# Macaron block with expert-choice feed-forward on one Trainium2 core: the first expert's weight halves made on ScalarE and GpSimd during the threshold search

## What is computed

```python
x = x + 0.5 * ffn(layernorm(x))
x = x + attention(layernorm(x))
x = x + 0.5 * ffn(layernorm(x))

# ffn (8 experts, 1024 hidden), "expert choice":
xn     = rmsnorm(x) * norm_weight
probs  = softmax(xn @ router_w.T + router_b)
gates, idx = top_k(probs.T, cap)          # cap = 2048 rows for each expert
hmid   = gelu(xn[idx] @ fc1_w[e].T + fc1_b[e])
ye     = hmid @ fc2_w[e].T + fc2_b[e]
out    = scatter_add(ye * gates) / scatter_add(gates)
```

## Time and profile before

| | us |
|---|---|
| median of 3 runs | 2071.78 (2070.72 to 2072.58) |
| the profiled execution | 2071.05 |
| its span, from first to last instruction | 2069.2 |
| PE busy | 1951.3 (94%) |
| DVE busy | 1449.0 (70%) |
| ACT busy | 1398.8 (68%) |
| POOL busy | 1259.4 (61%) |

### The profile page before, as it was taken

The page is one execution under the profiler, slowest core; times in us unless marked ns, Lnnn a source line. Parts: engine busy times, 40 slices in busy tenths (PEclk is TensorE's granted clock), DMA queues, the critical chain, the costliest instruction groups (busy, mean ns, idle before and its releaser), DMA issues. The chain is left out here.

```text
span 2069.2 us, 42505 instructions
## 1 busy us (share of the span) xinstructions
PE 1951.3 (94%) x15382; PEld 1352.3 (65%) x15382; DVE 1449.0 (70%) x4271; ACT 1398.8 (68%) x2680; POOL 1259.4 (61%) x1437
## 2 busy tenths in 40 slices
PE   8858999999999999799999999669999999999997
PEld 6534666666666666577777777435666666666665
DVE  7778777777777765488899998677555555656542
ACT  8635676766767676578888787455576676666663
POOL 8224887777777776644444442027877676767674
PEclk9979999999999999999999999989999999999999
DMA  9943565646565545655555554234655555646453
GB/s 289 346 123 92 114 101 91 106 89 131 85 108 92 100 76 69 116 134 154 159 159 163 135 150 116 85 77 105 107 115 89 107 108 87 131 85 106 71 77 36
DMA packets 361744, 242.33 MB, mean 117 GB/s; under 512 B 228928, under 2 KB 348992, under 8 KB 361280
## 3 DMA queue, kind: packets, MB, share of 16 engines
q1 hardware_dynamic: 304192, 172.34, 31.7%
q0 software_dynamic: 57344, 67.29, 22.4%
HBM read 121.03 MB, written 84.93 MB: 100 GB/s over the span
## 5 line engine op out<-in xcount | busy, mean ns | idle before, releaser
L1273 DVE SCALAR_TENSOR_TENSOR hid_l<-hf,hid_h 128x512 f16<-128x512 f32 x512 | 352.3, 699 | 341.4 <-ACT hid_h L719 340.0
L1494 PE MATMUL ps<-w_h,hid_h 128*128 128x256 f16 x2048 | 559.2, 273 | 0.0
L1495 PE MATMUL ps<-w_l,hid_h 128*128 128x256 f16 x2048 | 559.1, 273 | 0.0
L1496 PE MATMUL ps<-w_h,hid_l 128*128 128x256 f16 x2048 | 558.9, 273 | 0.0
L1494 PE MATMUL ps<-xt,w_h 128*128 128x512 f16 x1024 | 389.8, 381 | 19.4 <-ACT hf L820 14.3
L820 ACT ACTIVATE hf<-ps,b 128x512 f32<-128x512 f32 x512 | 345.1, 674 | 78.5 <-PE ps L1496 72.1
L1496 PE MATMUL ps<-xt,w_l 128*128 128x512 f16 x1024 | 389.9, 381 | 0.0
L1495 PE MATMUL ps<-xt,w_h 128*128 128x512 f16 x1024 | 389.7, 381 | 0.0
L719 ACT ACTIVATE ys<-yb,weight 128x256 f32<-128x256 f32 x256 | 128.0, 506 | 342.6 <-DVE yb L1291 336.2
L719 ACT ACTIVATE hid_h<-hf 128x512 f16<-128x512 f32 x512 | 322.5, 630 | 16.2
L606 POOL DMA_INDIRECT weight<-gate_d,gate_at x256 | 257.7, 1007 | 84.1 <-issue 76.5
(11 more groups left out here) (289 smaller groups left out, 3818.1 us busy)
## 6 DMA issues: line engine op xcount, KB each, us to landing
w_st<-fc_t SPq DMA_DIRECT2D x32, 1024.0 KB
xin<-x SPq DMA_DIRECT2D x32, 512.0 KB, 6.1
xa<-x_d SPq DMA_DIRECT2D x32, 512.0 KB, 4.6
out<-x SPq DMA_DIRECT2D x32, 512.0 KB, 5.2
z_d<-z SPq DMA_DIRECT2D x32, 512.0 KB, 6.1
xt<-xs SPq DMA_TRANSPOSE x256
weight<-gate_d,gate_at POOLq DMA_INDIRECT x256, 2.4
b_st<-fc_b SPq DMA_DIRECT2D x16, 128.0 KB
```

The costliest lines, as they stand in the source:

```text
L1273: dve.scalar_tensor_tensor(hid_l[:, n % 2, f, :], hf[:, f % HF, :], HS, hid_h[:, n % 2, f, :], ALU.mult, ALU.subtract).then_inc(s_hl, 1)
L1494: pe.matmul(dst, lh, rh, start=first, stop=False)
L1495: pe.matmul(dst, lh, rl, start=False, stop=False)
L1496: return pe.matmul(dst, ll, rh, start=False, stop=last)
```

## The change

The high halves of expert E0 are made by ACT inside the search: in rounds 8 and 9 the two parts of `fc1`, in rounds 10 to 13 the four parts of `fc2`, each behind that round's count. The low halves of E0 are made by POOL, as the first thing of its part of the layer, with two instructions for each part: a product by the scale into the loaded weights in place (linked, so POOL waits for its end), and a difference with the high half. The six copies leave ACT's program after the search, and the six low halves of E0 leave DVE's. The other experts are as before.

```diff
+    CONVERT = 8
@@ gpsimd
+            def first_lows(layer):
+                E = NE * layer
+                for k in range(KD):
+                    pool.wait_ge(s_w1h, KD * E + k + 1)
+                    steps.link(pool.tensor_scalar(w1_st[:, k, :], w1_st[:, k, :], nws[:, k:k + 1], None, ALU.mult))
+                    pool.tensor_tensor(w1_l[:, E % 2, k, :], w1_st[:, k, :], w1_h[:, E % 2, k, :], ALU.subtract).then_inc(s_w1, 1)
+                for h in range(4):
+                    pool.wait_ge(s_w2h, 4 * E + h + 1)
+                    part = slice(h * KF // 4, (h + 1) * KF // 4)
+                    steps.link(pool.tensor_scalar(flat(w2_st[:, part, :]), flat(w2_st[:, part, :]), WS, None, ALU.mult))
+                    pool.tensor_tensor(flat(w2_l[:, E % 2, part, :]), flat(w2_st[:, part, :]), flat(w2_h[:, E % 2, part, :]),
+                                       ALU.subtract).then_inc(s_w2, 1)
...
+            first_lows(0)
             ffn_rows(0, xf, x1_d)
...
+            first_lows(1)
             ffn_rows(1, z_d, outf)
@@ scalar, route
                     if i == 2:
                         copy(flat(p_r[:, :, :]), flat(ps[0][:, :, :])).then_inc(s_prr, 1)
+                    if CONVERT <= i < CONVERT + KD:
+                        w1_hi(NE * layer, i - CONVERT)
+                    if CONVERT + KD <= i < CONVERT + KD + 4:
+                        w2_hi(NE * layer, i - CONVERT - KD)
@@ scalar, ffn
                 act.activation(warm[:, :], nws[:, 0:1], ACT.Gelu)
-                for k in range(KD):
-                    w1_hi(E0, k)
-                for h in range(4):
-                    w2_hi(E0, h)
@@ vector, ffn
                 count_slots(0, E0, 0)
-                w1_lo(E0, 0)
                 tiles(0, E0, 1, NC)
                 count_slots(0, E0, 1)
                 rows_stats(N0, 0, 2)
-                if layer == 0:
-                    w1_lo(E0, 1)
                 rows_shift(N0, 0, 2)
                 rows_stats(N0, 2, TG)
                 rows_lo(N0, 0, 2)
-                if layer == 1:
-                    w1_lo(E0, 1)
...
                 choice_2(layer)
-                for h in range(4):
-                    w2_lo(E0, h)
                 rows_stats(N0 + 1)
```

More of the change, by code:

```diff
@@ L756, in _, with w1_hi, w2_hi @@
                     exponents(0, (g - 16) // 10)
+            def w1_hi(E, k):
+                if k == 0:
+                    act.wait_ge(s_w1d, 16 * (E + 1))
+                    wait(act, s_h, KF * NC * (E - 1))
+                copy(w1_h[:, E % 2, k, :], w1_st[:, k, :], scale=nws[:, k:k + 1]).then_inc(s_w1h, 1)
+            def w2_hi(E, h):
+                if h == 0:
+                    act.wait_ge(s_w2d, 16 * (E + 1))
+                    wait(act, s_y, TG * NC * (E - 1))
+                part = slice(h * KF // 4, (h + 1) * KF // 4)
+                copy(w2_h[:, E % 2, part, :], w2_st[:, part, :], scale=WS).then_inc(s_w2h, 1)
             def route(layer):
@@ L823, in gelu @@
                     copy(hid_h[:, n % 2, f, :], hf[:, f % HF, :], scale=HS).then_inc(s_hh, 1)
[L825 to L836, removed]
                 def y_out(n, t):
```

## The result

The changed kernel takes 2088.22 us, median of 4 runs (2086.22 to 2088.40), against 2072.18 (2070.72 to 2072.95, 4 runs) for the kernel before on the same chip: a ratio of 1.0075 with a 95% interval from 1.0059 to 1.0091. It is 16 us slower. The forecast was 2092, with a range from 2077 to 2103 and 0.88 on slower, so time and sign came as forecast. Part of that is luck: POOL worked half as long again as I had put down and held less of the loop than I had assumed, and the two errors nearly cancelled. The profiled execution has a span of 2086.4 us, 17.2 above before.

A forecast was written before the change was run, and what follows sets the result against it. The search's DVE and PE loop bounds its second half, PE nearly all the rest. On the profiled 2071.05 us, +22.0 stalls +3.0 clock -4.3 gain = 2091.75; with the median 0.73 above that execution, about 2092, range 2077 to 2103.

The forecast's parts named there:

- What bounds the kernel: In the search's second half one loop through DVE and PE sets the time, 2.67 us a round; elsewhere PE is nearly full.
- ACT's part: Six copies, 4.7 us a layer, fit ACT's idle 1.43 us in each search round; cost on the loop 0.
- POOL's length: POOL's products and differences beside the search take 13.5 us a layer, and their length alone delays nothing.
- rival (d): POOL is still in the low halves when the rows are listed after the search, so gathers are late; chance 0.01.
- What POOL does to DVE: In the search loop, POOL instructions reading SBUF hold some DVE forms until their end: 11.0 us a layer, 22.0 for both.
- the walk: Laying POOL's work on search rounds: round 8 +1.0, round 9 +4.4, rounds 10 to 13 +1.4 each; 11.0 us a layer.
- rival (c): POOL's product in the search costs as much as two-input arithmetic: 15.7 us a layer, 2102 in all; chance 0.11.
- The clock: PE idles in stretched search rounds and its clock drops: 0.3 us for each of five rounds, 3.0 in all.
- The gain: DVE loses the low halves behind the search: 1.1 and 2.5 us in layer 0, 0.7 in layer 1, 4.3 together.
- Next late are the second group's transposes: In layer 0, without `w2_lo` before the second group's statistics, 2.5 us is gained, as the transposes move with it.
- (a): POOL's instructions don't hold the search loop, so only the gain is left: 2067.5, faster by 0.2%; chance 0.10.
- (b): Only `short` and `cand` are held in the search, the masks pass: 6.8 us a layer, 2081 to 2084; chance 0.16 with mixtures.

The follow-up runs named there:

- e1_high_only: Changed kernel's high halves by ACT inside the search, but low halves left on DVE as in the kernel before, nothing new for POOL: 2071.95 us, ratio 1.0001.
- e5_price: Kernel before plus a test behind its end, timing POOL's product and difference alone and beside short DVE instructions: run once, 2140.41 us.
- e7_roots_sooner: e6_lows_in_wait with POOL's roots of the second group moved ahead of the third group's last two gathers: 2069.64 us, ratio 0.9995.
- after_again: The changed kernel run again, unaltered, for a second profile: 2089.97 us, ratio 1.0083.
- e6_lows_in_wait: Against the kernel before: high halves by ACT in the search, low halves by DVE in its waits for PE there, nothing for POOL: 2070.72 us, ratio 0.9997.
- e8: Changed kernel with ACT making the products too, POOL only the six differences, fc1's high halves moved to rounds 3 and 5: 2090.09 us, ratio 1.0083.
- e3_differences: e1_high_only plus POOL's six differences in each layer, written to an idle tile that nothing reads: 2086.80 us, ratio 1.0074.

## Why the prediction was right, and which of its steps were not

**What bounds the kernel, and ACT's part: right.** The loop of the search was the place: the searches take 19.7 us more (9.25 + 10.42), the whole span 17.2. ACT's copies cost 0 (e1_high_only).

**POOL's length: wrong for the product.** Difference 2.13 and 1.17 forecast, 2.12 and 1.15 to 1.21 measured. Product 1.05 and 0.62 forecast, 2.93 and 1.49 measured, above even the upper bounds of 2.34 and 1.17. The mis-sized term is the product's price. I had taken the slope of a cast, "since it has one input as they have". e5_price shows what the number of inputs does not tell: the multiplication costs 2.8 us where the copy costs 1.04. POOL works 20.9 us a layer instead of 13.5. It ends at 130.58, still 2.5 us before `thr_m`, so rival (d) stayed away, with less room than forecast.

**What POOL does to DVE: right in kind, wrong in one half.** The differences hold `short`, `cand` and the masks' form for their whole length, as the two rows of the trace before had it. The products hold these forms only in parts. Round by round against the forecast: round 8 3.54 (3.7 forecast), round 9 5.13 (7), round 10 4.60 and round 12 4.62 (4), round 11 3.46 (4), round 13 2.97 (4). Round 9 was over-priced: its first difference started after the masks and not in front of them, since the product before it was 1.9 us longer, and it fell on `short`. At the true length of the products and with the whole of each held, the walk would have exceeded rival (c)'s 15.7 us a layer (an argument from the walk, not a run). What was measured is 9.25 and 10.42. The mis-sized product (+7.4 us of POOL work) and the hold assumed whole took each other out.

**The clock: right in kind, and of the forecast's size or a little above.** Rounds 10 to 12 of layer 0 ran at 0.57, 0.50 and 0.69, where before had 0.63 and 0.82 in rounds 11 and 12 (the first in the earlier trace rows). In three rounds the slow clock can be read without a held mask beside it: PE's sums took 1.82 us in round 10 of layer 0 and 1.89 in rounds 10 and 13 of layer 1, in place of 1.11. The last of them, from the timeline of after:

```profile
1362.12 1.89 PE L1595 MATMUL ps<-masks,same_two 128*128 128x64 f16 x32 [1.05 <-DVE masks L1110]
```

In that round the masks, the next candidates, `short` and `cand` all keep their usual times, and it is 3.46 us long, 0.79 more than 2.67. The three make 2.3 us. The second halves of the sums in rounds 12 and 14 of layer 0 (1.03 and 1.00 us in place of 0.64) add 0.7. Round 11 of layer 0 and round 14 of layer 1 have sums of 1.89 us beside held masks; for them I estimate 1.5 from where the masks end. That is some 4.5 us, of which before paid 0.8 in its own two long rounds. So of the 19.7 us some 16 are left for POOL's holds, where the forecast had 22.0, and 3.7 for the clock, where it had 3.0 (estimates).

**The gain: too high.** The forecast was 4.3 us, that is 3.6 in layer 0 and 0.7 in layer 1.
- Layer 0, to fc1: 1.1 forecast, 1.11 measured (26.81 to 25.70). The cause is less sure than the number, for e1_high_only, which moves only ACT's copies, already gave 0.86 there and took it back in the second group. 
- Layer 0, second group: 2.5 forecast, 1.16 measured. "Next late are the second group's transposes" was the failed step. Next late was POOL's queue, two gathers that stand in front of the root (e7_roots_sooner got 1.04 of it back). The two parts together, which are steadier, give 2.3 of the 3.6 that were forecast. PE's gap that I expected to fall from 3.17 to 0.6 us fell to 2.12:

```profile
167.54 0.39 PE L1503 MATMUL ps<-xt,w_h 128*128 128x512 f16 x1 [2.12 <-ACT hf L853]
```

- Layer 1: 0.7 forecast, a loss of 0.95 measured, and 0.73 in after_again. The row halves are ready 0.4 and 0.6 us sooner than in before, so DVE did gain; but from there to the first product it takes 5.5 us in both, against 4.1 in before, 4.5 in e6_lows_in_wait and 2.7 in e7_roots_sooner. This time is the transposes' landing. Why they land later in the changed kernel stays open; that DVE's low halves are gone is not enough, for they are gone in e6, e7 and e8 too, whose fc1 comes 21.29, 21.42 and 22.07 us behind the search, against 22.82 and 22.60 in the changed kernel.

Put together on the profiled span: 9.25 + 10.42 - 1.11 - 1.16 + 0.95 = 18.4 us, and the stretches outside give back 1.1 (1.0 before the first search, 0.6 behind the last start, less 0.5 between), which makes the 17.2 within rounding. The forecast had 25.0 of stall and clock and 4.3 of gain, 20.7. Both terms were too large, by 5.3 and by 3.0.

**The rivals.** (a), no hold, and (b), the masks pass, are disproved by e3_differences and e5_price. (c) had the price of the product too low rather than too high and was still above the measured time, because the price isn't what counts: it is the time for which a form is held. The time lies between (b)'s 2084 and the forecast's 2092, about half way. In the term itself it is nearer to (b): the searches grew by 19.7 us, where (b) had 13.6, and up to 16.6 with the clock, and the forecast 25.0. Still (b)'s mechanism is not what happened, since the masks are held.

## What to carry to other kernels

POOL is not a free engine beside a latency loop on DVE: a POOL instruction on SBUF is priced by what it holds and when it starts, and the loop's short instructions out of SBUF pay for it, up to one whole POOL instruction at a time. Before giving POOL elementwise work, look for a row of that very operation and not of one with as many inputs; here they differ by 2.7 times. If DVE has a wait of its own in the loop, a piece cut to the length of that wait costs next to nothing there (e6_lows_in_wait), but taking work away behind the loop pays only as far as the next engine's queue allows.

## What the runs showed of the hardware

- A float32 product by a scalar on POOL takes 2.8 to 2.9 us for 128x1024 and 1.53 for 128x512, slower than the two-input difference (2.12 and 1.15) and 2.7 times the copy (1.04). 
- The product of 1024 elements holds DVE in phases: two-input and one-input forms to 1.1 us, nothing from 1.1 to 1.8, one-input forms alone from 1.8 to the end. The difference holds all SBUF forms for its whole 2.12 us. Reductions out of PSUM were never held. 
- Fills on POOL, 1.1 us each, hold one-input forms of DVE though they read nothing; 17.5 us of them in layer 0 (8.87 + 6.48 + 2.17) cost 4.9 us of search. 
- The same six differences cost between 7.2 and 9.3 us a search. A hold also leaves PE idle: behind one of 2.14 us its next sums took 1.89 us in place of 1.11.
- A held DVE instruction is shown as busy: DVE was busy 12.5 us longer with 10 us less work.
